# Cross attention's probabilities: 32x32 blocks on VectorE and SBUF-to-SBUF transfers in place of TensorE transposes

## What is computed

```python
xn = _layernorm(x, ln_gamma, ln_beta)
q = (xn @ w_q).reshape(B, SQ, NUM_HEADS, DIM_HEAD)
kv = context @ w_kv
k, v = jnp.split(kv, 2, axis=-1)
scores = jnp.einsum('bqhd,bkhd->bhqk', q * SCALE, k)
attn = jax.nn.softmax(scores, axis=-1)
out = jnp.einsum('bhqk,bkhd->bqhd', attn, v).reshape(B, SQ, INNER)
```

## Time and profile before

| | us |
|---|---|
| median of 3 runs | 1898.67 (1897.55 to 1899.34) |
| the profiled execution's own time | 1897.99 |
| its span in the trace | 1896.2 |
| TensorE busy | 1857.4 (98%) |
| VectorE, ScalarE, GpSimd busy | 1039.5 (55%), 664.8 (35%), 559.2 (29%) |
| TensorE's granted clock, mean over the span | 0.996 of full speed |

### The profile page before, as it was taken

The page is one execution under the profiler, slowest core; times in us unless marked ns, Lnnn a source line. Parts: engine busy times, 40 slices in busy tenths (PEclk is TensorE's granted clock), DMA queues, the critical chain, the costliest instruction groups (busy, mean ns, idle before and its releaser), DMA issues.

```text
span 1896.2 us, 36612 instructions
## 1 busy us (share of the span) xinstructions
PE 1857.4 (98%) x14096; PEld 1604.4 (85%) x14096; DVE 1039.5 (55%) x2015; ACT 664.8 (35%) x1356; POOL 559.2 (29%) x546
## 2 busy tenths in 40 slices
PE   5989999999999999999999999999999999999999
PEld 4868988998998999899899989788887778888887
DVE  7615555555455555545554554688888743333322
ACT  3225444444444444444444444411111421111111
POOL 3016334433633443363344335431111000000000
PEclk9999999999999999999999999999999999999999
DMA  7323313322331332233133224733341321010000
GB/s 245 125 91 96 90 55 111 100 70 80 103 92 55 111 98 70 80 103 94 55 111 95 72 80 132 213 89 95 100 156 46 112 66 67 1 67 0 29 16 23
DMA packets 166485, 165.59 MB, mean 87 GB/s; under 512 B 8672, under 2 KB 123744, under 8 KB 166432
## 3 DMA queue, kind: packets, MB, share of 16 engines
q1 hardware_dynamic: 162000, 156.20, 27.2%
q10 hardware_dynamic: 4432, 8.65, 1.2%
HBM read 131.01 MB, written 33.82 MB: 87 GB/s over the span
## 4 chain that ended last, share of the span: by engine, by line
PE 90%; DVE 1%; DMA 1%; SPq 1%; POOL 0%; issue 0%; ACT 0%; ACTq 0%; DVEq 0%; POOLq 0%
PE s_ps L83 24%; PE s_ps L84 23%; PE s_ps L85 23%; PE s_ps L538 7%; PE s_ps L598 6%; PE s_ps L572 3%; PE s_ps L605 1%; PE s_ps L1265 1%; PE s_ps L1276 1%; PE s_ps L1207 0%; DMA a_xin<-x 0%; DMA a_m_xn<-x 0%; PE s_ps L1287 0%; PE s_ps L546 0%; PE s_ps L1256 0%
## 5 line engine op out<-in xcount | busy, mean ns | idle before, releaser
L494 POOL TENSOR_TENSOR x_prob<-x_prob,x_share 128x256 f32<-128x256 f32 x256 | 157.5, 615 | 596.0 <-DVE x_share L660 588.9
L83 PE MATMUL s_ps<-w_cT_hi,w_space_hi 128*128 128x258 f32 x1024 | 295.9, 289 | 0.0
L84 PE MATMUL s_ps<-w_cT_lo,w_space_hi 128*128 128x258 f32 x1024 | 290.5, 284 | 0.0
L85 PE MATMUL s_ps<-w_cT_hi,w_space_lo 128*128 128x258 f32 x1024 | 288.4, 282 | 0.0
L677 DVE COPY x_mix<-s_ps 128x512 f32<-128x512 f32 x256 | 176.7, 690 | 121.7 <-PE s_ps L85 121.7
L83 PE MATMUL s_ps<-x_pT_hi,x_cn_hi 128*128 128x512 f32 x512 | 206.4, 403 | 1.5 <-DVE x_mix L677 1.5
L767 ACT ACTIVATE x_prob<-s_ps,x_negmax 128x257 f32<-128x257 f32 x256 | 122.2, 477 | 226.7 <-DVE x_negmax L655 226.6
L85 PE MATMUL s_ps<-x_pT_hi,x_cn_lo 128*128 128x512 f32 x512 | 201.0, 393 | 0.0
L84 PE MATMUL s_ps<-x_pT_lo,x_cn_hi 128*128 128x512 f32 x512 | 199.8, 390 | 0.0
L655 DVE TENSOR_REDUCE x_negmax<-s_ps 128x1 f32<-128x257 f32 x256 | 108.2, 423 | 165.6 <-PE s_ps L85 165.6
L83 PEld LDWEIGHTS s_ps<-w_cT_hi,w_space_hi 128*128 128x128 f32 x1024 | 193.7, 189 | 2.0 <-issue 0.2
(11 more groups left out here) (205 smaller groups left out, 3547.0 us busy)
## 6 DMA issues: line engine op xcount, KB each, us to landing
e_raw_T<-ctx_T SPq DMA_DIRECT2D x64, 514.0 KB, 4.0
e_raw_n<-ctx_nat SPq DMA_DIRECT2D x64, 512.0 KB, 3.6
q<-q_q ACTq DMA_DIRECT2D x16, 512.0 KB, 2.8
e_q<-q SPq DMA_DIRECT2D x16, 512.0 KB, 4.2
o_hi<-x_o_hi SPq DMA_DIRECT2D x32, 256.0 KB, 3.0
o_lo<-x_o_lo SPq DMA_DIRECT2D x32, 256.0 KB, 3.5
a_oT_hi<-o_hi SPq DMA_DIRECT2D x16, 512.0 KB, 4.3
a_oT_lo<-o_lo SPq DMA_DIRECT2D x16, 512.0 KB, 5.6
```

The source lines that it names most:

```text
L83: pe.matmul(out, lhs[0], rhs[0], start=start, stop=False)
L84: pe.matmul(out, lhs[0], rhs[1], start=False, stop=False)
L85: return pe.matmul(out, lhs[1], rhs[0], start=False, stop=stop)
L494: pool.tensor_tensor(prob[:, i, 0:KT * P], prob[:, i, 0:KT * P], share[:, i:i + 1].to_broadcast([P, KT * P]), ALU.mult)\
```

## The change

TensorE's transposes and their PSUM banks are gone. VectorE turns each tile of `prob` in 32x32 blocks into a new tile `blocks` (`turn_tile`, 4 per batch, 128x256 each). That leaves each block's rows in the right order but on the wrong partitions; SyncE then moves them with four DMAs per batch (`exchange`) from the 32 partitions of a head group to all 128 partitions of `prob_T`, 128 KB each in runs of 512 bytes. `high_probs` and `split_probs` read `prob_T` in SBUF. The keys come out in another order than before, which the load of `raw_n` follows (`by_blocks`), and so do the heads' columns, which `out_half` follows (`place`). `exps` of a tile waits until the tile of the batch before has been turned. In the last turn part of the weight loads is issued later. Line numbers after the change are some 10 to 20 higher.

```diff
--- before.py
+++ after.py
@@ -337,6 +337,7 @@
     TILES = heads // HT
+    BLOCKS = KT * P // SQ
     HE = inner // heads
@@ -352,8 +353,10 @@
     o = s.pair("o", [P, PAIRS // 2, P])
+    blocks = s.sb("blocks", [P, BLOCKS, TILES, SQ])
+    prob_T = s.sb("prob_T", [P, KT, heads * SQ])
     negmax, total, share = s.sb("negmax", [P, TILES]), s.sb("total", [P, TILES]), s.sb("share", [P, TILES])
-    S_BANK, T_BANK, M_BANK = (0, 1, 2, 5), (3, 4), (6, 7)
+    S_BANK, M_BANK = (0, 1, 2, 5), (6, 7)
     O_BANK = (6, 7)
@@ -370,7 +373,8 @@
     last_ready, last_turned = s.count("last_ready", GB), s.count("last_turned", 1)
-    turned = s.count("turned", GB * KT)
+    turned = s.count("turned", GB * TILES)
+    moved = s.count("moved", 16 * HT * GB)
     pT_hi, pT_lo = s.count("pT_hi", GB * KT), s.count("pT_lo", GB * KT)
@@ -391,6 +395,10 @@
+    def place(h):
+        at = h % HT * TILES + h // HT
+        return slice(at * SQ, (at + 1) * SQ)
+
     def of_head(a, h):
@@ -400,8 +408,15 @@
         def load_n(t, b):
-            sp.dma_start(raw_n[:, :, :], ctx_nat[t * GB + b, 0:KT * P, :].rearrange("(k p) d -> p k d", p=P))\
+            sp.dma_start(raw_n[:, :, :], ahead.by_blocks(ctx_nat[t * GB + b, 0:KT * P, :]))\
                 .then_inc(n_loaded.sem, 16)
+
+        def exchange(t, b):
+            sp.wait_ge(turned.sem, turned.at(t, (b + 1) * TILES))
+            for g in range(HT):
+                sp.dma_start(prob_T[:, :, g * P:(g + 1) * P],
+                             blocks[g * SQ:(g + 1) * SQ, :, :, :].rearrange("p (m k) i n -> p m k (i n)", k=KT))\
+                    .then_inc(moved.sem, 16)
 
@@ -431,18 +446,19 @@
             load_v(t)
-            if not more:
-                load_w(range(PAIRS + 2))
             if more:
                 sp.wait_ge(fold_ready.sem, fold_ready.at(t, PAIRS))
                 load_q(t, 1)
             for b in range(GB - 1):
+                exchange(t, b + 1)
                 if b + 2 < GB or more:
                     sp.wait_ge(nlo_done.sem, nlo_done.at(t, b + 2))
                     load_n(t, b + 2)
                 if more:
                     sp.wait_ge(Tlo_done.sem, Tlo_done.at(t, b + 4))
                     load_T(t, b + 4)
+                elif b < 2:
+                    load_w(range(b * (PAIRS + 2) // 2, (b + 1) * (PAIRS + 2) // 2))
             if not more:
@@ -450,6 +466,7 @@
             if more:
+                exchange(t, GB)
                 sp.wait_ge(nlo_done.sem, nlo_done.at(t, GB + 1))
...
@@ -565,14 +583,6 @@
-        def turn_probs(t, b):
-            for i in range(TILES):
-                pe.wait_ge(probs_ready.sem, probs_ready.at(t, b * TILES + i + 1))
-                for k in range(KT):
-                    mm = pe.transpose(ps[:, T_BANK[k], i * P:(i + 1) * P], prob[:, i, k * P:(k + 1) * P], ident[:, :])
-                    if i == TILES - 1:
-                        mm.then_inc(turned.sem, 1)
-
         def mix_chunk(t, b, c):
@@ -595,7 +605,7 @@
                         n = 2 * j + h
-                        pe.matmul(out[h], w_v[:, c, n * HE:(n + 1) * HE], mix[:, c, :, n * SQ:(n + 1) * SQ],
+                        pe.matmul(out[h], w_v[:, c, n * HE:(n + 1) * HE], mix[:, c, :, place(n)],
                                   start=c == 0, stop=False)
@@ -608,18 +618,14 @@
             for b in range(GB - 1):
-                turn_probs(t, b)
                 scores(t, b + 1)
                 if b < GB - 2:
                     for c in range(DC):
                         mix_chunk(t, b, c)
-            mix_chunk(t, 2, 0)
-            mix_chunk(t, 2, 1)
-            turn_probs(t, 3)
-            mix_chunk(t, 2, 2)
-            mix_chunk(t, 2, 3)
+            for c in range(DC):
+                mix_chunk(t, 2, c)
             if more:
-                pe.wait_ge(pT_lo.sem, pT_lo.at(t, GB * KT))
+                pe.wait_ge(exp_done.sem, exp_done.at(t, GB * TILES))
                 for j in range(3):
@@ -659,17 +665,25 @@
+        def turn_tile(t, b, i):
+            dve.wait_ge(probs_ready.sem, probs_ready.at(t, b * TILES + i + 1))
+            dve.transpose(blocks[:, :, i, :], prob[:, i, 0:KT * P].rearrange("p (k n) -> p k n", n=SQ))\
+                .then_inc(turned.sem, 1)
+
         def softmax(t, b):
+
             for i in range(TILES):
                 row_max(t, b, i)
                 if i > 0:
                     invert(t, b, i - 1)
+                if i > 1:
+                    turn_tile(t, b, i - 2)
             invert(t, b, TILES - 1)
 
         def split_probs(t, b):
             for k in range(KT):
                 dve.wait_ge(pT_hi.sem, pT_hi.at(t, b * KT + k + 1))
-                dve.tensor_tensor(pT[b % 2][1][:, k, :], ps[:, T_BANK[k], :], f32(pT[b % 2][0][:, k, :]), ALU.subtract)\
+                dve.tensor_tensor(pT[b % 2][1][:, k, :], prob_T[:, k, :], f32(pT[b % 2][0][:, k, :]), ALU.subtract)\
                     .then_inc(pT_lo.sem, 1)
@@ -703,14 +717,12 @@
                 softmax(t, b + 1)
-                if b < GB - 2:
-                    for c in range(DC):
-                        keep_mix(t, b, c)
-            keep_mix(t, 2, 0)
-            keep_mix(t, 2, 1)
+                turn_tile(t, b + 1, 2)
+                keep_mix(t, b, 0)
+                turn_tile(t, b + 1, 3)
+                for c in range(1, DC):
+                    keep_mix(t, b, c)
             split_probs(t, 3)
-            keep_mix(t, 2, 2)
-            keep_mix(t, 2, 3)
             if more:
...
@@ -762,15 +778,19 @@
             act.wait_ge(max_done.sem, max_done.at(t, b * TILES + i + 1))
-            if i == 0 and b > 0:
-                act.wait_ge(last_ready.sem, last_ready.at(t, b))
+            if b > 0:
+                act.wait_ge(turned.sem, turned.at(t, (b - 1) * TILES + i + 1))
+                if i == 0:
+                    act.wait_ge(last_ready.sem, last_ready.at(t, b))
             act.activation(prob[:, i, 0:SK], ps[:, S_BANK[i], 0:SK], ACT.Exp,
                            bias=negmax[:, i:i + 1], accum_out=total[:, i:i + 1]).then_inc(exp_done.sem, 1)
 
         def high_probs(t, b):
+            if b >= 2:
+                act.wait_ge(mixed.sem, mixed.at(t, (b - 1) * DC))
+            act.wait_ge(moved.sem, moved.at(t, 16 * HT * (b + 1)))
             for k in range(KT):
-                act.wait_ge(turned.sem, turned.at(t, b * KT + k + 1))
-                act.activation(pT[b % 2][0][:, k, :], ps[:, T_BANK[k], :], ACT.Copy).then_inc(pT_hi.sem, 1)
+                act.activation(pT[b % 2][0][:, k, :], prob_T[:, k, :], ACT.Copy).then_inc(pT_hi.sem, 1)
 
@@ -868,8 +888,13 @@
         self.raw_n = s.sb("raw_n", [P, KT, dim])
-        self.n_src = ctx_nat[0, 0:KT * P, :].rearrange("(k p) d -> p k d", p=P)
+        self.n_src = self.by_blocks(ctx_nat[0, 0:KT * P, :])
         self.q = s.sb("q", [P, PAIRS, turn])
+
+    @staticmethod
+    def by_blocks(rows):
+
+        return rows.rearrange("(m k e) d -> e m k d", m=4, k=2)
 
```

More of the change, by code:

```diff
@@ L470, in sync @@
             load_T(0, b + 1)
+        exchange(0, 0)
         sp.wait_ge(nlo_done.sem, nlo_done.at(0, 1))
@@ L732, in turn @@
                 softmax(t, GB)
+                turn_tile(t, GB, 2)
+                turn_tile(t, GB, 3)
             else:
@@ L744, in vector @@
         softmax(0, 0)
+        turn_tile(0, 0, 2)
+        turn_tile(0, 0, 3)
         dve.wait_ge(v_stored, 16)
```

## The result

| | us, median | interval or range |
|---|---|---|
| before, beside the change | 1898.21 | 1897.55 to 1899.34 |
| after | 1907.78 | 1905.20 to 1908.57 |
| ratio | 1.0047 | 1.0032 to 1.0062 |

Slower by 0.5%, more than the 0.2% that can be told from nothing. The forecast was 1868. The profiled span is 1906.0 us, 9.8 over the 1896.2 of before.

A forecast was written before the change was run, and what follows sets the result against it. TensorE bounded the kernel before; afterwards the loop would, at 48.5 + 4E = 64.5 us a turn against 66.43. 1.9 us less over 15.5 turns is 30 us: 1898.0 - 30 = 1868 us, range 1842 to 1918.

The forecast's parts named there:

- the bound: Before the change TensorE, busy 98% of the span, bounds the kernel; only time taken from it counts.
- the removal: Eight transposes per batch leave TensorE: 0.87 us for each of 64 batches, 56 us, the most that can be won.
- the loop: Split, row maxima, block turns and transfer form a closed loop over VectorE, SyncE and DMA: 10.99 us a batch, 64.5 a turn.
- The floor: TensorE's own work without the transposes: a turn of 62.95 us, 1842 us in all.
- landing to row maximum: Loop leg from a transfer's landing, through ScalarE's copies, to the next row maximum on VectorE: 1.94 us.
- row maximum to last block turn: Loop leg from a batch's first row maximum to the end of its last block turn on VectorE: 5.05 us.
- Its ends of -16 and +21 us: Range for a block turn of 256 columns, 0.30 to 0.60 us against 0.43 taken, two per batch on the path.
- E: Loop leg from the last block turn's end to the last of four DMA landings: 4.0 us, between 3.3 and 5.5.
- 15.5 turns with the same gain: Each turn gains 1.9 us, over 15.5 turns since the last has no folds: 30 us.
- The query load's collision: Batch 1's transfer meets the next turn's query load on the DMA queue: 1.0 us a turn, from 0 to 3.2.
- The slow transfer: Rival at the four DMAs of `exchange`: 32 source partitions halve the rate, E 4.9, 1924 us; chance 0.26.
- The lock of VectorE and GpSimd: Rival: VectorE's subtraction in `split_probs` meets GpSimd's work, 0.5 us four times a turn, 1899 us; chance 0.04.

The follow-up runs named there:

- order2: The change with ScalarE's high parts right behind the next softmax's first exponential and VectorE's split behind its second row maximum: 1875.50 us, ratio 0.9875.
- both: The change with order2's edit, and the next fold pair 0's high and low parts ahead of batch 3's high parts and split: 1864.45 us, ratio 0.9813.

## Why the prediction was wrong

- **Right: the bound, the removal, the loop.** L572 is gone. TensorE's busy time fell by 35 us, not 56 to 68; without the transfer it fell by 51. A matmul that starts behind a wait counts longer: the mean of the mixture's L83 rose from 403 to 414 ns. The floor is 62.90 a turn (62.95 forecast), the legs landing to row maximum 1.87 (1.94) and row maximum to last block turn 4.94 to 5.02 (5.05), a block turn 0.42 to 0.45 us (0.43). Its ends of -16 and +21 us were not needed. That the copies read SBUF now costs 0.03 us each and stays hidden.
- **Wrong in size: E, the step that failed.** I took 4.0 from the pair of output stores, whose issues are 0.46 apart. Measured 4.8 to 5.0, mean 4.9. Three issues of 0.67 are 0.63 us over three of 0.46; and with three of 0.46 an E of 4.0 leaves 2.5 for the last landing, which takes 2.7 to 2.8. Another row was nearer: the query load's single issue takes 0.59, and I had used it only for its collision. But the output stores too have pieces of 512 bytes, so the size of the pieces does not tell which row is the right one. Nor do the bytes: the issue of `raw_n` took 0.37 us before and 0.63 in the reordered form, with the same 512 KB in runs of 2 KB. What makes an issue 0.4 or 0.6 us stays open; one dimension less and 128 source partitions changed nothing. In 14 turns the miss is 14 x (66.52 - 64.5) = 28 us, of the 40 between forecast and result.
- **Wrong in scope: 15.5 turns with the same gain.** The prologue's softmax and the last turn have no folds or output beside the transfer, so it stands bare: TensorE waits 2.99 us for the first `pT_lo` and 3.61 for the last. Forecast for one and a half turns -2.9, measured +8.8: the other 12 us. In the last turn the transfer is not all of it: without it that turn is still 69.72 against 68.29 before, and TensorE waits 2.25 and 0.68 us there, 1.9 of it by the meeting of VectorE and GpSimd.
- **The query load's collision** was 0.2 us in the profiled turn and 0.3 in the mean, not 1.0. That is no rule for quicker transfers: with 128 source partitions it was 1.0 and with three transfers 0.8, so the forecast's price would have held for an E near 4. With the four E as measured, which hold it already, the sum is 47.5 + 19.6 = 67.1 a turn, 0.6 over the measured 66.5. The traces show where: from the high parts to the next batch's last block turn are 6.81 to 6.89 us, three times, and not 6.99, and 26.44 over the folds and not 26.53. The two errors of the turn's sum are then +2.6 by E and the collision together and -0.6 here.
- **The rivals.** The slow transfer had the right place, sign and E (4.9), but that number was in part luck. Its reason, half the rate from 32 partitions, is the smaller part, 0.6 us of E by the run with 128, and its lower end took 1.4 us of data in a 2.8 us store, which no row shows. The Trainium skill, page "SBUF — State Buffer", section "Door 1: The DMA port swizzle", by which 32 partitions reach 8 of 16 ports, is borne out in kind by that run. The lock of VectorE and GpSimd does not occur in the change (688 ns a subtraction). It does without the transfer (936) and in order2 and both (835 and 830), in the loop without a loss that shows in the turn, but with 1.9 us in the last turn without the transfer.
- **What would show it.** The waits came in the three places named, chunk 2, `mix_chunk(3, 0)` and fold pair 5 (the row at 666.09), but with 3.7 us a turn and not 1.5. "Wrong if TensorE waits for the context rows" did not occur: they land after 4.0 us, and no wait of TensorE names them.

## What to carry to other kernels

A row of DMAs has a price of its own on the issuing queue. It can't be taken from any other issue at hand, since the ones in this trace take from 0.37 to 0.67 us without a reason that bytes or piece size give: take the dearest as the upper end, or measure. With four legs in a turn and sixteen turns each 0.1 us is worth 6 us. When a step goes from a quick engine to a slow path, look what stands in the same queues behind the wait for it: here an order of the steps that fills the wait gave 43 us, more than any change to the transfer that was tried, short of leaving it out. And count the first and the last turn apart, since they lack the cover.

## What was not expected of the hardware

- One issue on SyncE takes 0.34 us for 32 pieces of 16 bytes, and 0.61 to 0.67 for 256 pieces of 512 bytes. The load of 512 KB of context rows takes 0.37 in its old form and 0.63 in the reordered one.
- Two queues issue at the same time, but the landing of a 128 KB piece grows from 2.7 to 3.3 and 3.5 us, so most of the gain is given back.
- The same 128 KB land in 2.2 us from 128 partitions and in 2.7 from 32.
- VectorE's subtraction of two SBUF tiles that starts while GpSimd works on SBUF tiles ends 0.55 us after GpSimd's instruction: 65 times of 65 without the transfer, 47 of 47 in order2. With one source in PSUM (before, 48 times) it takes its usual 0.69 us.
